# Attention on one core: probability transposes ahead of a group's first projections, the last query block's scores behind the projections

## The chip, the cores and the metric

The kernel runs on one core of a Trainium2 chip. The metric is the device time of one execution in microseconds; the lower, the better. The engines that matter here are TensorE (PE in the profile; its weight loads are PEld), VectorE (DVE), ScalarE (ACT), GpSimd (POOL) and SyncE (SP), which issues the loads.

## What is computed

One decoder layer in float32: self-attention, a cross-attention with a given context, and a mixture of experts. The change touches the self-attention alone:

```python
def proj(W):
    y = jnp.einsum('bsh,oh->bso', hidden_states, W)
    return y.reshape(B, S, NH, HD).transpose(0, 2, 1, 3)
q, k, v = (proj(Wq), proj(Wk), proj(Wv))
q = q * cos + rotate_half(q) * sin
k = k * cos + rotate_half(k) * sin
scores = jnp.einsum('bhqd,bhkd->bhqk', q, k) / math.sqrt(HD)
scores = jnp.where(causal, -jnp.inf, scores)
attn = jax.nn.softmax(scores, axis=-1)
out = jnp.einsum('bhqk,bhkd->bhqd', attn, v)
```

The batch is 4, the sequence 1024, the width 1024, with 16 heads of 64. `x` is normalised before it.

## The kernel before

`self_attention` works through 4 batches of 8 pairs of heads. Each engine has one queue, written by hand, and works it in order; semaphores tie the queues together. For every batch a `prologue` turns `x` and makes the first pair's projections. Then `attention` runs once for each pair, eight times in a batch: the first pair, three passes of a hardware loop (`pe.Fori`) with two pairs each, and the last pair. While it weighs the values of pair j it makes the projections of pair j + 1, except in the last pair of a batch. So 28 of the 32 calls have projections in them; these are the "pairs with projections" below.

Values are split in two float32r summands (`_hi` and `_lo`): ScalarE writes `_hi`, VectorE or GpSimd writes `_lo` as the rest, and TensorE multiplies both.

A pair has 24 steps, `STEPS[s] = (u, kb)`: unit u is a head and a half of the queries (`u` 0 to 3; two units see 4 key blocks of 128, two see 8), kb is the key block. A step does the following on TensorE, in this order:

- it turns the probabilities of key block kb (2 to 4 transposes, 1 at the diagonal's end; L433), to bank `ps_t`. ScalarE copies them to `pt_hi` (L556) and VectorE makes `pt_lo` (L707);
- it makes the scores of one query block of a later unit (`next_queries`, `scores`, L373 to L377), to `ps_s`. VectorE takes the row maxima (L659), ScalarE the exponentials (L494) and the normalisation (L502);
- it weighs the values (L417, L418) with the transposes of the step before. In the third step of a group this comes behind the projections.

Three steps are a group (`PER = 3`, `group, place = divmod(s, PER)`), and group t makes the projection of token block t of the next pair. Its 24 matmuls, 8 weight blocks k of 128 rows with three terms each (L347), are cut in `PARTS`: 12 at place 0, 6 at place 1 and 6 at place 2. All go to the one bank `ps_qkv`. When the last is done, ScalarE copies the value part (L481), and VectorE runs `rotate` (L632, L635, L636, L637, L642). The first projection of the next group waits for `qkv_read`, which L637 gives. At place 1 the rotated queries and keys of the block before are turned (L361), copied by ScalarE (L485) and split by VectorE (L650, L651).

In group 0 two more things happen. The weights of the next pair are only now being split: ScalarE writes `w_hi` (L472) of blocks 4 and 5 in step 0 and of blocks 6 and 7 in step 1 (`W_OF_STEP`), each block followed by `w_lo` on GpSimd (L276, `rest_of_w`), and the projections wait for it block by block:

```python
k, term = divmod(n, 3)
if t == 0 and term == 0:
    pe.wait_ge(w_lo_ok, START + j * HB + k + 1)
```

And the scores of step 2 are those of the last query block of unit 1. They need token block 7 of this pair's queries and keys, which is turned in step 1, so they wait for L651.

Of the kernel before, what the change touches and what calls it, by code (L numbers as in the profile page):

```python
# [113 lines left out]
def self_attention(nc, const, x, wqkv, cos, sin, attn_out):  # L114
# [10 lines left out]
    STEPS = [(u, kb) for u in range(NU) for kb in range(KB[u])]  # L125
    NS = len(STEPS)
    PER = NS // TB
# [12 lines left out]
    def next_queries(s, last):  # L140

        u, kb = STEPS[s]
        if KB[u] == GQ:
            then = [(u + 1, kb + 1)] if kb + 1 < GQ else []
        else:
            then = [(u + 1, kb // 2)] if kb % 2 == 0 else [(u + 2, 0)] if kb == KB[u] - 1 else []
        return [(unit // NU, unit % NU, i) for unit, i in then if unit < NU or not last]

    def tile_order(last):


        order = []
        for s in range(NS):
            order.append(("probs", s))
            if s % PER == 1 and (s < PER or not last):
                order.append(("qk", s // PER))
        return {key: i for i, key in enumerate(order)}

    with ExitStack() as scope:
# [46 lines left out]
        def first_tile(j):  # L206

            return j * NT + TB - 1
# [120 lines left out]
        def _(pe):  # L329
# [8 lines left out]
            def qkv(j, t, part, out):  # L338

                for n in part:  # L340
# [4 lines that stand above are left out]
                    a = slice(t * P, (t + 1) * P)  # L345
                    xs, ws = ((xt_hi, w_hi), (xt_hi, w_lo), (xt_lo, w_hi))[term]
                    mm = pe.matmul(out, xs[:, k, a], ws[:, k, :], start=(n == 0), stop=(n == 3 * HB - 1))  # L347
                    if t == TB - 1 and n == 3 * SLOTS - 1:

                        mm.then_inc(w_early, 1)  # L350
                if part[-1] == 3 * HB - 1:
                    mm.then_inc(qkv_ok, 1)

            def turn_qk(j, t, start, at):


                pe.wait_ge(rot_ok, START + j * TB + t + 1)

                pe.wait_ge(tile_lo_ok, START + (start + (at - 1 if at >= 2 else 0)))
                for r in range(4):  # L360
                    mm = pe.transpose(ps_t[:, at % 2, r * P:(r + 1) * P], rotated[:, r, :, :].rearrange("p a d -> p (a d)"), ident[:, :])  # L361
                mm.then_inc(tile_ok, 1)

            def scores(j, slot, u, i):
                h, g = UNITS[u]
                n = GQ * u + i
                qb = GQ * g + i
                keys = P * (qb + 1)
                for c in range(0, keys, BANK):

                    w = max(min(BANK, keys - c), 2 * P)
                    out = ps_s[:, n % 2, c:c + w]
                    pe.matmul(out, qk_hi[slot][:, h, qb * P:(qb + 1) * P], qk_hi[slot][:, 2 + h, c:c + w],  # L373
                              start=True, stop=False, skip_group_check=True)
                    pe.matmul(out, q_lo[slot][:, h, qb * P:(qb + 1) * P], qk_hi[slot][:, 2 + h, c:c + w],
                              start=False, stop=True, skip_group_check=True)
                mm = pe.matmul(ps_s[:, n % 2, qb * P:(qb + 1) * P], ident16[:, :], mask16[:, :],  # L377
                               start=False, stop=True, skip_group_check=True)
                mm.then_inc(s_ok, 1)
# [27 lines left out]
            def weigh_values(j, slot, s, tile):  # L407
                u, kb = STEPS[s]
                h, g = UNITS[u]

                pe.wait_ge(tile_lo_ok, START + tile)
                if kb == 0:

                    pe.wait_ge(o_ok, START + j * NU + u)
                off = P * max(0, kb - GQ * g)
                both = v[slot][:, kb, h, :, :].rearrange("p a d -> p (a d)")
                pe.matmul(ps_o[:, off:], both, pt_hi[:, s % 2, off:], start=(kb == 0), stop=False, skip_group_check=True)  # L417
                pe.matmul(ps_o[:, off:], both, pt_lo[:, s % 2, off:], start=False, stop=True,  # L418
                          skip_group_check=True).then_inc(pv_ok, 1)

            def attention(j, slot, first, last):
                tiles = tile_order(last)
                for s, (u, kb) in enumerate(STEPS):
                    h, g = UNITS[u]
                    group, place = divmod(s, PER)
                    if kb == 0:

                        pe.wait_ge(norm_ok, START + j * NQ + GQ * (u + 1))
                    at = tiles["probs", s]

                    pe.wait_ge(tile_lo_ok, START + first_tile(j) + (at - 1))
                    for i in range(max(0, kb - GQ * g), GQ):
                        mm = pe.transpose(ps_t[:, (TB - 1 + at) % 2, i * P:(i + 1) * P], probs[g][:, i, kb * P:(kb + 1) * P], ident[:, :])  # L433
                    mm.then_inc(tile_ok, 1)
                    for ahead, unit, i in next_queries(s, last):

                        if unit == 1 and not ahead:
                            pe.wait_ge(tile_lo_ok, START + (first_tile(j) + (tiles["qk", 0] + 1 if i == GQ - 1 else 0)))
                        elif unit == 1:
                            pe.wait_ge(tile_lo_ok, START + first_tile(j) + tiles["qk", GQ + 1] + 1)  # L440
                        elif unit == 0 and i == 0:
                            pe.wait_ge(tile_lo_ok, START + first_tile(j) + tiles["qk", GQ] + 1)

                        pe.wait_ge(exp_ok, START + (j + ahead) * NQ + GQ * unit + i - 1)
                        scores(j + ahead, (slot + ahead) % 2, unit, i)
                    if 0 < s and place < PER - 1:
                        weigh_values(j, slot, s - 1, first_tile(j) + tiles["probs", s - 1] + 1)
                    elif s == 0 and not first:
                        weigh_values(j - 1, 1 - slot, NS - 1, first_tile(j))
                    if place == 1 and group == 0:  # L450
                        turn_qk(j, TB - 1, j * NT, TB - 1 + tiles["qk", 0])
                    elif place == 1 and not last:
                        turn_qk(j + 1, group - 1, j * NT, TB - 1 + tiles["qk", group])
                    if not last:
                        if place == 0:

                            pe.wait_ge(qkv_read, START + j * TB + TB + group)
                        qkv(j + 1, group, PARTS[place], ps_qkv[:, 0:W])
                    if place == PER - 1:

                        weigh_values(j, slot, s - 1, first_tile(j) + tiles["probs", s - 1] + 1)

            def drain(j):
                weigh_values(j, 1, NS - 1, (j + 1) * NT)

            for_pairs(pe, prologue, attention, drain)

        @block.scalar
# [1655 lines left out]
```

## Time and profile before

| what | value |
| --- | --- |
| median of 3 runs (lowest to highest) | 7976.89 us (7974.31 to 7977.77) |
| the profiled execution's own time | 7973.0 us |
| its span | 7971.4 us |
| TensorE busy in the span | 7279.0 us (91%) |
| VectorE, ScalarE, GpSimd busy | 4039.8, 3494.3, 1726.8 us |
| attention, from the first pair's first step to the last batch's end | 83.0 to 2519.8 us of the span |
| TensorE busy in that stretch | 2194.49 us |
| a pair with projections, 850.5 to 920.1 us | 69.60 us |

Start times count from the start of the span. A busy time of TensorE contains the time that a matmul takes to run through the array: a 128x384 matmul is shown with 0.33 us, yet the next one starts 0.17 us after it. So waits are read best from the distance between starts, and a wait shorter than the run-through does not show as idle time on PE; the row of the weight load (PEld) may show it. "Clock 1.00" in a row is the full 2.4 GHz, 0.50 is 1.2 GHz.

### The profile page before, as it was taken

How to read it: one execution, taken by the hardware profiler on the slowest of the kernel's cores; microseconds unless marked ns; L12 is line 12 of the kernel's file. 1: busy time of each engine (PE TensorE's matmuls, PEld its weight loads, DVE VectorE, ACT ScalarE, POOL GpSimd, SP SyncE). 2: the span in 40 equal slices, each digit the busy share in tenths (PEclk: the TensorE clock that was granted, in tenths of full speed). 3: DMA queues.
4: the chain of work that ended last, by engine and by line, in shares of the span. 5: the costliest groups of instructions: out<-in, count | busy, mean ns of one | idle time of the engine just before them, and what ended most of it. 6: DMA issues, size and time to landing. Idle time of an engine off the chain costs nothing.

```text
span 7971.4 us, 127669 instructions
## 1 busy us (share of the span) xinstructions
PE 7279.0 (91%) x39854; PEld 6170.5 (77%) x39856; DVE 4039.8 (51%) x8063; ACT 3494.3 (44%) x6664; POOL 1726.8 (22%) x1646
## 2 busy tenths in 40 slices
PE   8998997997996988994899999999999999999999
PEld 7887886886885777773777888877887878887887
DVE  6666666666665444345444444444444444444444
ACT  5665665665665122110344444444444444444443
POOL 1111111111110000000233333333333333333333
PEclk9998998998998999996899999999999999999999
DMA  1101111111102111211455555555555555555555
GB/s 58 32 25 51 27 31 43 32 32 43 32 25 81 64 67 64 93 56 39 134 163 153 155 154 154 155 158 157 155 153 172 150 163 155 155 153 157 154 155 145
DMA packets 286465, 826.59 MB, mean 104 GB/s; under 512 B 35872, under 2 KB 103456, under 8 KB 286112
## 3 DMA queue, kind: packets, MB, share of 16 engines
q0 software_dynamic: 98928, 365.58, 18.9%
q1 hardware_dynamic: 187184, 456.61, 17.5%
q8 instruction: 185, 3.03, 0.2%
q14 instruction: 168, 1.38, 0.1%
HBM read 615.37 MB, written 206.70 MB: 103 GB/s over the span
## 4 chain that ended last, share of the span: by engine, by line
PE 44%; DMA 2%; issue 2%; DVE 1%; DVEq 1%; ACT 1%; POOLq 0%; ACTq 0%; POOL 0%
PE ps_gu L1612 9%; PE ps_gu L1614 9%; PE ps_gu L1613 9%; PE ps_y L1612 4%; PE ps_y L1614 4%; PE ps_y L1613 4%; PE ps_xe L1632 3%; DMA xt_rows<-rows,gather_t 2%; PE ps_xe L1641 1%; DVEq L1482 1%; PE ps_l L1621 1%; DVE gu_lo L1972 1%; POOLq L1482 0%; ACT y_last L1774 0%; ACT xs_hi L1757 0%
## 5 line engine op out<-in xcount | busy, mean ns | idle before, releaser
L1612 PE MATMUL ps_gu<-xs_hi,gu_hi 128*128 128x512 f32 x3072 | 1232.2, 401 | 95.0 <-DVE gu_lo L1972 95.0
L1614 PE MATMUL ps_gu<-xs_hi,gu_lo 128*128 128x512 f32 x3072 | 1213.0, 395 | 0.0
L1613 PE MATMUL ps_gu<-xs_lo,gu_hi 128*128 128x512 f32 x3072 | 1209.8, 394 | 0.0
L1612 PEld LDWEIGHTS ps_gu<-xs_hi,gu_hi 128*128 128x128 f32 x3072 | 583.0, 190 | 240.9 <-DVE gu_lo L1972 122.5
L347 PE MATMUL ps_qkv<-w_hi,xt_hi 128*128 128x384 f32 x1920 | 711.3, 370 | 51.9 <-DVE v L637 51.9
L1591 POOL TENSOR_TENSOR dn_lo<-raw_w,dn_hi 128x512 fp32r<-128x512 f32 x384 | 485.2, 1298 | 1007.8 <-ACT dn_hi L1793 1007.8
L1614 PEld LDWEIGHTS ps_gu<-xs_hi,gu_lo 128*128 128x128 f32 x3072 | 582.9, 190 | 131.1
L1613 PEld LDWEIGHTS ps_gu<-xs_lo,gu_hi 128*128 128x128 f32 x3072 | 583.2, 190 | 122.3
L707 DVE TENSOR_TENSOR pt_lo<-ps_t,pt_hi 128x512 fp32r<-128x512 f32 (+3 forms) x768 | 425.3, 554 | 451.7 <-ACT pt_hi L556 438.8
L347 PE MATMUL ps_qkv<-w_hi,xt_lo 128*128 128x384 f32 x1920 | 653.3, 340 | 0.0
L347 PE MATMUL ps_qkv<-w_lo,xt_hi 128*128 128x384 f32 x1920 | 651.5, 339 | 0.0
L1612 PE MATMUL ps_y<-dn_hi,hs_hi 128*128 128x512 f32 x1536 | 628.5, 409 | 0.0
L1972 DVE TENSOR_TENSOR gu_lo<-raw_w,gu_hi 128x512 fp32r<-128x512 f32 x768 | 485.1, 686 | 263.5 <-ACT gu_hi L1793 262.4
L1932 DVE TENSOR_TENSOR xs_lo<-ps_xe,xs_hi 128x512 fp32r<-128x512 f32 x520 | 334.6, 685 | 549.9 <-ACT xs_hi L1757 549.9
L1614 PE MATMUL ps_y<-dn_hi,hs_lo 128*128 128x512 f32 x1536 | 606.7, 395 | 0.0
L1613 PE MATMUL ps_y<-dn_lo,hs_hi 128*128 128x512 f32 x1536 | 606.2, 395 | 0.0
L1805 ACT ACTIVATE hs_hi<-act_s 128x512 fp32r<-128x512 f32 x192 | 121.3, 632 | 1096.6 <-DVE act_s L1977 1096.6
L1977 DVE TENSOR_TENSOR act_s<-ps_gu,act_s 128x512 f32<-128x512 f32 x192 | 132.9, 692 | 925.2 <-PE ps_gu L1614 925.2
L556 ACT ACTIVATE pt_hi<-ps_t 128x512 fp32r<-128x512 f32 (+3 forms) x768 | 374.9, 488 | 342.8 <-PE ps_t L433 324.9
L1569 POOL DMA_INDIRECT out<-y_sup,scatter_s x192 | 303.5, 1581 | 1003.7 <-ACT y_sup L1815 980.3
L1793 ACT ACTIVATE gu_hi<-raw_w 128x512 fp32r<-128x512 f32 x768 | 426.0, 618 | 184.2 <-DMA raw_w<-w_gu 184.2
L1815 ACT ACTIVATE y_sup<-ps_y,w_now 128x512 f32<-128x512 f32 x384 | 264.6, 689 | 437.8 <-PE ps_y L1614 422.5
(303 smaller groups left out, 16328.8 us busy)
## 6 DMA issues: line engine op xcount, KB each, us to landing
raw_w<-w_gu SPq DMA_DIRECT2D x384, 512.0 KB, 4.1
raw_w<-w_down SPq DMA_DIRECT2D x192, 512.0 KB, 6.7
w_raw<-wqkv SPq DMA_DIRECT2D x260, 192.0 KB, 2.5
out<-residual SPq DMA_DIRECT2D x36, 512.0 KB, 2.6
probs<-x SPq DMA_DIRECT2D x32, 512.0 KB, 3.4
attn_out<-out_t POOLq DMA_DIRECT2D x128, 128.0 KB, 2.2
residual<-x SPq DMA_DIRECT2D x32, 512.0 KB, 4.2
stage<-attn_out SPq DMA_DIRECT2D x32, 512.0 KB, 5.1
```

What stands on the lines that cost most here:

```text
L347: mm = pe.matmul(out, xs[:, k, a], ws[:, k, :], start=(n == 0), stop=(n == 3 * HB - 1))
L556: act.activation(pt_hi[:, s % 2, off:], ps_t[:, (TB - 1 + at) % 2, off:], ACT.Copy).then_inc(tile_hi_ok, 1)
L707: dve.tensor_tensor(pt_lo[:, s % 2, off:], ps_t[:, (TB - 1 + at) % 2, off:], raw(pt_hi[:, s % 2, off:]), ALU.subtract).then_inc(tile_lo_ok, 1)
L1569: pool.indirect_dma_start(out, bass.IndirectOffsetOnAxis(ap=scatter_s[:, i:i + 1], axis=0), y_sup[:, i % 2, :], None, compute_op=ALU.add). ...
L1591: pool.tensor_tensor(dn_lo[:, f, a], raw_w[:, f, a], raw(dn_hi[:, f, a]), ALU.subtract).then_inc(dn_lo_ok, 1)
L1612: pe.matmul(out, a_hi, w_hi, start=first, stop=False)
L1613: pe.matmul(out, a_hi, w_lo, start=False, stop=False)
L1614: return pe.matmul(out, a_lo, w_hi, start=False, stop=last)
L1793: act.activation(dst[:, a], raw_w[:, c % RING, a], ACT.Copy).then_inc(hi_ok, 1)
L1815: act.activation(y_sup[:, i % 2, a], ps_y[:, a], ACT.Copy, scale=w_now[:, i:i + 1]).then_inc(ys_ok, 1)
L1932: dve.tensor_tensor(xs_lo[:, ks, a], ps_x1[:, c * BANK:(c + 1) * BANK].rearrange("p (k c) -> p k c", c=P), raw(xs_hi[:, ks, a]), ALU.subtr ...
L1972: dve.tensor_tensor(gu_lo[:, c // 2, b], raw_w[:, c % RING, a], raw(gu_hi[:, c // 2, b]), ALU.subtract).then_inc(lo_ok, 1)
```

## The change

The body of `attention` on TensorE gets two local functions, `turn_probs(s)` (the transposes) and `next_scores(s)` (the scores), with the same instructions as before. Two orders change, both in the 28 pairs with projections:

- `turned_early(s)`: the transposes of the second step of a group are issued in the first step, ahead of the group's 12 first projections and of their wait for `qkv_read`. That holds for six of the eight groups (steps 1, 7, 10, 13, 19, 22). Steps 4 and 16 start a unit (kb = 0) and stay.
- `late_scores`: in step 2 the scores go behind the six projections, so that they come between these and the weighing of values.

The queues of the other engines are the same as before, instruction by instruction.

```diff
@@ -420,9 +420,10 @@
 
             def attention(j, slot, first, last):
                 tiles = tile_order(last)
-                for s, (u, kb) in enumerate(STEPS):
+
+                def turn_probs(s):
+                    u, kb = STEPS[s]
                     h, g = UNITS[u]
-                    group, place = divmod(s, PER)
                     if kb == 0:
 
                         pe.wait_ge(norm_ok, START + j * NQ + GQ * (u + 1))
@@ -432,6 +433,8 @@
                     for i in range(max(0, kb - GQ * g), GQ):
                         mm = pe.transpose(ps_t[:, (TB - 1 + at) % 2, i * P:(i + 1) * P], probs[g][:, i, kb * P:(kb + 1) * P], ident[:, :])
                     mm.then_inc(tile_ok, 1)
+
+                def next_scores(s):
                     for ahead, unit, i in next_queries(s, last):
 
                         if unit == 1 and not ahead:
@@ -443,6 +446,18 @@
 
                         pe.wait_ge(exp_ok, START + (j + ahead) * NQ + GQ * unit + i - 1)
                         scores(j + ahead, (slot + ahead) % 2, unit, i)
+
+                def turned_early(s):
+
+                    return not last and s % PER == 1 and STEPS[s][1] > 0
+
+                for s, (u, kb) in enumerate(STEPS):
+                    group, place = divmod(s, PER)
+                    if not turned_early(s):
+                        turn_probs(s)
+                    late_scores = group == 0 and place == PER - 1 and not last
+                    if not late_scores:
+                        next_scores(s)
                     if 0 < s and place < PER - 1:
                         weigh_values(j, slot, s - 1, first_tile(j) + tiles["probs", s - 1] + 1)
                     elif s == 0 and not first:
@@ -454,8 +469,12 @@
                     if not last:
                         if place == 0:
 
+                            if turned_early(s + 1):
+                                turn_probs(s + 1)
                             pe.wait_ge(qkv_read, START + j * TB + TB + group)
                         qkv(j + 1, group, PARTS[place], ps_qkv[:, 0:W])
+                    if late_scores:
+                        next_scores(s)
                     if place == PER - 1:
 
                         weigh_values(j, slot, s - 1, first_tile(j) + tiles["probs", s - 1] + 1)
```

On TensorE's queue, step 2 of a pair in the loop: `ps_t<-ident,probs` are the transposes, `ps_s` the scores, `ps_qkv` the projections, of weight blocks 6 and 7 here. Before:

```order
L433 MATMUL ps_t<-ident,probs 128x128 x2
L438 REGISTER_ALU
L444 REGISTER_ALU
L373 MATMUL ps_s<-qk_hi 128x512
L375 MATMUL ps_s<-qk_hi,q_lo 128x512
L373 MATMUL ps_s<-qk_hi 128x512
L375 MATMUL ps_s<-qk_hi,q_lo 128x512
L377 MATMUL ps_s<-mask,ident 128x128
L344 REGISTER_ALU
L347 MATMUL ps_qkv<-w_hi,xt_hi 128x384
L347 MATMUL ps_qkv<-w_lo,xt_hi 128x384
L347 MATMUL ps_qkv<-w_hi,xt_lo 128x384
```

And after the change:

```order
L434 MATMUL ps_t<-ident,probs 128x128 x2
L344 REGISTER_ALU
L347 MATMUL ps_qkv<-w_hi,xt_hi 128x384
L347 MATMUL ps_qkv<-w_lo,xt_hi 128x384
L347 MATMUL ps_qkv<-w_hi,xt_lo 128x384
L344 REGISTER_ALU
L347 MATMUL ps_qkv<-w_hi,xt_hi 128x384
L347 MATMUL ps_qkv<-w_lo,xt_hi 128x384
L347 MATMUL ps_qkv<-w_hi,xt_lo 128x384
L441 REGISTER_ALU
L447 REGISTER_ALU
L373 MATMUL ps_s<-qk_hi 128x512
```

The projections of block 6 and, three rows on, of block 7 (each with its wait for `w_lo_ok`) now stand ahead of the scores.

On the same queue, steps 6 and 7 of the pair: `ps_o` is the weighing of values, and the register operation ahead of the projections belongs to the wait for `qkv_read`. Before:

```order
L411 REGISTER_ALU
L417 MATMUL ps_o<-pt_hi,v 128x512
L418 MATMUL ps_o<-pt_lo,v 128x512
L457 REGISTER_ALU
L347 MATMUL ps_qkv<-w_hi,xt_hi 128x384
L347 MATMUL ps_qkv<-w_lo,xt_hi 128x384
...
L347 MATMUL ps_qkv<-w_hi,xt_lo 128x384
L433 MATMUL ps_t<-ident,probs 128x128 x4
L411 REGISTER_ALU
L417 MATMUL ps_o<-pt_hi,v 128x512
```

And after the change:

```order
L411 REGISTER_ALU
L417 MATMUL ps_o<-pt_hi,v 128x512
L418 MATMUL ps_o<-pt_lo,v 128x512
L434 MATMUL ps_t<-ident,probs 128x128 x4
L474 REGISTER_ALU
L347 MATMUL ps_qkv<-w_hi,xt_hi 128x384
L347 MATMUL ps_qkv<-w_lo,xt_hi 128x384
...
L347 MATMUL ps_qkv<-w_hi,xt_lo 128x384
L411 REGISTER_ALU
L417 MATMUL ps_o<-pt_hi,v 128x512
```

The four transposes of step 7 moved from behind the twelve projections to ahead of them and of their wait. Steps 9 and 10 read the same way with two transposes, steps 18, 19 and 21, 22 repeat them in the second half.

## Rows read from the trace of the kernel before

**Rows 1.** Who waited for whom, 0 to 2560 us: total us, times, longest.

```profile
PEld ps_qkv L347 <- DVE v L637: 106.1, 168, 1.0
...
PE ps_o L417 <- DVE out_t L671: 30.3, 22, 2.4
PE ps_s L373 <- DVE qk_hi L651: 29.5, 29, 1.4
...
PEld ps_qkv L347 <- POOL w_lo L276: 0.9, 3, 0.4
```

**Rows 2.** Windows: length, busy of five engines, clock, DMA share, GB/s.

```profile
850.50:920.10 69.60, 66.57 (x408) 59.60 (x408) 47.92 (x117) 47.17 (x102) 10.44 (x12) 1.00 0.12 31
2318.20:2390.80 72.60, 68.28 (x409) 61.17 (x409) 47.24 (x114) 46.48 (x100) 10.25 (x12) 0.98 0.11 29
436.80:510.70 73.90, 69.64 (x408) 61.78 (x408) 47.14 (x114) 46.21 (x100) 10.10 (x12) 0.95 0.10 28
2325.00:2328.50 3.50, 2.86 (x10) 2.57 (x11) 2.15 (x4) 3.48 (x8) 1.97 (x2) 0.60 0.19 56
```

**Rows 3.** Timeline of PE, steps 6 and 7: start, length, instruction.

```profile
870.42 0.39 PE L418 MATMUL ps_o<-pt_lo,v 128*128 128x512 f32 x1
870.99 0.34 PE L347 MATMUL ps_qkv<-w_lo,xt_hi 128*128 128x384 f32 x1
...
872.73 0.34 PE L347 MATMUL ps_qkv<-w_hi,xt_lo 128*128 128x384 f32 x1
872.91 0.60 PE L433 MATMUL ps_t<-ident,probs 128*128 128x128 f32 x4
873.26 0.48 PE L417 MATMUL ps_o<-pt_hi,v 128*128 128x512 f32 x1
873.58 0.39 PE L418 MATMUL ps_o<-pt_lo,v 128*128 128x512 f32 x1
873.81 0.60 PE L361 MATMUL ps_t<-ident,rotated 128*128 128x128 f32 x4
```

**Rows 4.** Timeline of PE, steps 9 and 10 of the same pair.

```profile
878.30 0.40 PE L418 MATMUL ps_o<-pt_lo,v 128*128 128x512 f32 x1
878.86 0.45 PE L347 MATMUL ps_qkv<-w_hi,xt_hi 128*128 128x384 f32 x1 [0.16 <-DVE v L637]
879.15 0.34 PE L347 MATMUL ps_qkv<-w_lo,xt_hi 128*128 128x384 f32 x1
...
880.88 0.34 PE L347 MATMUL ps_qkv<-w_hi,xt_lo 128*128 128x384 f32 x1
881.06 0.38 PE L433 MATMUL ps_t<-ident,probs 128*128 128x128 f32 x2
...
881.51 0.40 PE L375 MATMUL ps_s<-qk_hi,q_lo 128*128 128x512 f32 x1
```

**Rows 5.** Timeline of PE, steps 2 and 3 of the same pair.

```profile
857.39 0.38 PE L433 MATMUL ps_t<-ident,probs 128*128 128x128 f32 x2
858.89 0.49 PE L373 MATMUL ps_s<-qk_hi 128*128 128x512 f32 x1 [1.11 <-DVE qk_hi L651]
...
859.91 0.23 PE L377 MATMUL ps_s<-mask,ident 128*128 128x128 bf16 x1
859.95 0.42 PE L347 MATMUL ps_qkv<-w_hi,xt_hi 128*128 128x384 f32 x1
...
861.67 0.28 PE L418 MATMUL ps_o<-pt_lo,v 128*128 128x256 f32 x1
862.76 0.44 PE L347 MATMUL ps_qkv<-w_hi,xt_hi 128*128 128x384 f32 x1 [0.81 <-DVE v L637]
```

**Rows 6.** Timeline of POOL, 850 to 864 us: the rests of weight blocks.

```profile
858.27 1.97 POOL L276 TENSOR_TENSOR w_lo<-w_raw,w_hi 128x384 fp32r<-128x384 f32 x2 [1.63 <-ACT w_hi L472]
```

**Rows 7.** Timeline of DVE, step 2: maxima, then rotation.

```profile
860.28 1.21 DVE L659 TENSOR_REDUCE neg_max<-ps_s 128x1 f32<-128x1024 f32 x1
861.69 0.42 DVE L632 TENSOR_TENSOR r_cos<-ps_qkv,cos_sb 128x256 f32<-128x256 f32 x1 [0.19 <-ACT v L481]
```

## The prediction

> **What bounds the kernel now.** I read first the table of who waited for whom, cut to the attention stretch, because the change moves waits and adds no work. It shows which waits TensorE has left [rows 1]. Its first projections of a group wait for the rotation, which frees `ps_qkv`: 168 waits of a weight load, 106.1 us, six in each of the 28 pairs with projections. The scores of step 2 wait for L651 29 times, 29.5 us in all. For the weights' rests on GpSimd it hardly waits at all: 3 times, 0.9 us. That row is the one to keep in mind, because it is a cover and not a freedom.
>
> Then the windows [rows 2]. A pair takes 69.60 us, of which TensorE is busy 66.57, so the stage is TensorE's own work plus short waits, and what can be won is those waits. Pairs behind a jump of the hardware loop are longer and have a lower clock: 0.98 and 0.95.
>
> Last the timelines of one pair at full clock, where I take the distance from start to start. Without a wait, the matmul behind L418 (512 columns) starts 0.23 us after it (873.58 to 873.81), and a projection 0.17 us after another [rows 3].
>
> **Transposes ahead, steps 6 and 7 (and 18 and 19).** From L418 at 870.42 to the second projection at 870.99 there are 0.57 us; without a wait it would be 0.23 + 0.17 = 0.40 [rows 3]. So the wait costs 0.17. Where the transposes stand now, from the last projection (872.73) over them to L418 (873.58), there are 0.85 us; without them the way is 0.17 + 0.23 = 0.40. Taking them away there saves 0.45. In front they need the 0.23 behind L418, 0.35 for themselves (872.91 to 873.26), and about 0.26 to the second projection (an estimate between 0.17 and the 0.28 that a projection behind a wait takes to the next): 0.84 instead of 0.57, so 0.27 is paid. Net 0.18, which is the wait. The bounds are 0.17 and 0.28.
>
> **Steps 9 and 10 (and 21 and 22).** Here L418 at 878.30 to the second projection at 879.15 is 0.85 us, a wait worth 0.45 [rows 4]. Two transposes take at most the 0.35 of four, so they vanish in it whole, and the projections start as before. Behind, 880.88 to the second scores at 881.51 is 0.63, against 0.17 + 0.23 = 0.40 without them: 0.23 saved.
>
> **Steps 0 and 1, 12 and 13.** Same move, but I count 0. The rows of waits give six waits for the rotation to a pair, and eight groups; the two groups in which other work already covers it are these two by their place behind the scores of a whole block. Transposes in front cost there what they save behind. Steps 3 and 15 have the long waits (below), but their next transposes start a unit and do not move, so nothing fills them.
>
> The early transposes add no wait of their own: they need the bank that L707 has read, and the weighing of values just ahead of them needs the same L707. ScalarE's copies of them can only come sooner.
>
> Sum of this part: 2 x 0.18 + 2 x 0.23 = 0.82 us a pair, 28 pairs: 23 us gained.
>
> **What a rule would make of it.** The transposes of rows 3 start 0.11 us apart. The Trainium skill, "TensorE: Matmul & The Clock Gate", section "Back-to-back issue gap", gives N/2.4 + 2.5 ns for isolated matmuls at full clock, 56 ns at 128 columns. By it, two transposes would hide 0.11 us instead of 0.23, and the part would bring an estimated 0.56 us a pair, 16 us. The rows have the duration of this very form, so I stay with them.
>
> **Scores behind the projections, step 2.** Now the transposes start at 857.39, the scores at 858.89 after an idle 1.11 us, their last matmul (the mask) at 859.91, the projections at 859.95 [rows 5]. It looks as if the six projections, some 1.04 us, would fit that hole. But they are of weight blocks 6 and 7, and they wait for `w_lo_ok`. GpSimd makes these two rests from 858.27 on, 1.97 us together, and was itself idle until ScalarE gave it the `w_hi` [rows 6]: the first is ready at about 859.26, the second at 860.24. Before the change the wait for L651 and the scores covered this: the projections of block 6 started at 859.95, 0.7 us after their weights.
>
> After the change, with the weights at the same times: block 6 starts at about 859.3, block 7 not before 860.3. From there 0.28 + 0.17 + 0.17 us to the first score matmul [rows 3] gives 860.9, although L651 would have let it go at 858.89. The mask comes 0.23 x 4 behind (the spacing of 512 columns), at about 861.9 instead of 859.91.
>
> What is queued behind: VectorE's row maxima of 1024 keys. They start 0.37 us after the mask and last 1.21 [rows 5, 7]; behind them on the same queue stands the rotation (L632), and behind its L637 the first projection of group 1, 1.07 us after L632 starts (861.69 to 862.76). So: 861.9 + 0.37 + 1.21 = 863.4 for L632, less a few hundredths of overlap, and 864.5 for the projection instead of 862.76. TensorE has only the weighing, one transpose and the weighing again to do meanwhile, which now end at 861.67 [rows 5] and would end near 862.5. Each pair loses 864.50 - 862.76 = **1.74 us**.
>
> Bounds: a gain of 0.2 if the weights came early enough, because then L632 would start with the end of the maxima at 861.49 and not at 861.69; a loss of 2.0 if the whole delay of the mask went through. The value comes from the chain, since each link has a row. Nothing later takes it up: TensorE is the engine that others follow from step 4 on.
>
> Three pairs are like the one with clock 0.95 [rows 2]: I take it that their step 2 runs partly at half clock and their rotation is late already, and count nothing for them. 25 x 1.74 = 43.5 us lost.
>
> **Sum.** 43.5 - 23 = 20.5 us slower. The profiled execution's own time is 7973.0 us, 3.9 below the median of the runs shown; 7973.0 + 20.5 + 3.9 = 7997.4. I predict 7997 us.
>
> **Rivals.**
> 1. *The clock falls in the new waits* (later than 8008). In step 2 TensorE now stands still from 857.5 (the second transpose, 0.11 us behind 857.39) to 859.3, and ahead of group 1 from 862.5 to 864.5: 1.8 and 2.0 us, where it stood 1.4 and 1.1. The longest wait for L671 was 2.4 us [rows 1], and in the window just behind such a one the clock is 0.60 [rows 2]. Against it: the pair at 850.5 has waits of 1.4 us and clock 1.00. The price: TensorE is busy 68.28 us in a pair with clock 0.98 against 66.57, 1.7 us; ten such pairs are 17 us, all 28 are 48. The Trainium skill, same page, section "Part 4: PE-mode transpose", says that transposes do not count as busy for the clock gate; by that rule the transposes placed beside these waits would not help the clock, and it speaks for this rival; no row of this trace tells transposes apart there. Chance 0.18.
> 2. *Loss and gain nearly cancel* (7961 to 7993). If ScalarE and GpSimd run 0.7 us earlier in step 1, since its transposes are there sooner, the delay shrinks to 1.0 us: 25 - 23 = 2 us slower. Against it: GpSimd waits 1.63 us for ScalarE ahead of those blocks, so it is ScalarE that would have to be faster, and its queue has the exponentials and copies ahead in the same order. Chance 0.18.
> 3. *Faster* (below 7961). The wait for the weights does not come because block 7 is ready when its projections are. Then step 2 brings 0.2 us a pair, 5 us, and the first part its 23: 7977 - 28 = 7949. It decides at one point: the rest of block 7 must be done by about 858.1 (857.5 + 0.6), and the row has 860.24. For a gain over 16 us with the first part alone the delay must stay under 0.25 us a pair. Chance 0.09.
>
> **Numbers.** My forecast (7990 to 8008) has 0.55. A measurement of this kernel tells 0.2%, 16 us, from no change. Of the forecast's range a small piece lies under +16 us: slower 0.55 - 0.05 + 0.18 = 0.68, same 0.23, faster 0.09. The range for 8 in 10 takes in most of rivals 1 and 2: 7974 to 8028. Its lower end is a delay of 0.8 us a pair, its upper end 18 pairs with a lower clock.
>
> **What the trace after would show.** The row "PEld ps_qkv L347 <- POOL w_lo L276" rises from 0.9 us to some 40 or more, with about two waits a pair. The wait of L373 for L651 goes from 29 times to four or so, those of the last pairs. The waits for L637 fall to about four a pair and grow at group 1. The pair that took 69.60 us takes 70.5. Steps 6, 7 and 9, 10 show no or a shorter wait at the projections. I am wrong if the weights' wait stays small, if group 1's projection is not late, or if the clock in pairs without a jump leaves 1.00.

## The result and the profile after

The changed kernel takes 8007.12 us (median of 6 runs, 7996.88 to 8008.32) against 7976.9 us (6 runs, 7974.01 to 7986.96): 1.0035 times the time before, with a 95% interval of 1.0024 to 1.0047. That ratio is 28 us; the two medians lie 30 us apart. Its profiled execution took 7996.88 us, the shortest of the six and 23.9 us more than the profiled one of before.

Between these two profiled executions all of the difference lies in attention. The first matmul of the next stage starts at 2589.33 us of the span; it started at 2565.02. That is 24.3 us, and behind it the two programs take the same (5406.0 and 5406.4 us). In the kernel after, L637 has become L656, L651 L670, L659 L678, L632 L651, L433 L434, L472 L491; the lines of the attention's other matmuls have kept their numbers. Some kernels of the experiments have a few lines more: in the timelines of stand_in_weights and rests_last L350 and L349 are L347, L376 and L375 (with `ps_s<-qk_hi`) are L373, and the L659 that two waits for the rotation name is L637.

The table of who waited for whom, 0 to 2600 us of the changed kernel (total us, times, longest), answers to [rows 1]:

```profile
PEld ps_qkv L347 <- DVE v L656: 78.7, 112, 1.7
PEld ps_qkv L347 <- POOL w_lo L276: 65.1, 63, 1.9
...
PE ps_o L417 <- DVE out_t L690: 35.1, 24, 2.6
...
PE ps_s L373 <- DVE qk_hi L670: 5.4, 4, 1.4
```

The waits for the rotation fall from 168 to 112, four a pair, but the longest grows from 1.0 to 1.7 us. The scores' wait is left only in the four last pairs. In its place stands the wait for the weights' rests on GpSimd: 65.1 us where there was 0.9. The wait for the rotation and that of the scores have lost 27.4 and 24.1 us, and the new wait has brought 64.2.

The same pair as in [rows 5], PE's timeline of steps 2 and 3; the pair starts at 859.20 instead of 850.52:

```profile
866.03 0.38 PE L434 MATMUL ps_t<-ident,probs 128*128 128x128 f32 x2
868.00 0.45 PE L347 MATMUL ps_qkv<-w_hi,xt_hi 128*128 128x384 f32 x1 [1.59 <-POOL w_lo L276]
...
868.98 0.44 PE L347 MATMUL ps_qkv<-w_hi,xt_hi 128*128 128x384 f32 x1 [0.18 <-POOL w_lo L276]
...
869.62 0.40 PE L373 MATMUL ps_s<-qk_hi 128*128 128x512 f32 x1
...
870.55 0.23 PE L377 MATMUL ps_s<-mask,ident 128*128 128x128 bf16 x1
...
871.25 0.28 PE L418 MATMUL ps_o<-pt_lo,v 128*128 128x256 f32 x1
873.02 0.44 PE L347 MATMUL ps_qkv<-w_hi,xt_hi 128*128 128x384 f32 x1 [1.49 <-DVE v L656]
```

And POOL's and DVE's timelines there, which answer to [rows 6, 7]:

```profile
866.96 1.96 POOL L276 TENSOR_TENSOR w_lo<-w_raw,w_hi 128x384 fp32r<-128x384 f32 x2 [1.63 <-ACT w_hi L491]
...
870.82 1.23 DVE L678 TENSOR_REDUCE neg_max<-ps_s 128x1 f32<-128x1024 f32 x1 [1.76 <-PE ps_s L377]
871.96 0.41 DVE L651 TENSOR_TENSOR r_cos<-ps_qkv,cos_sb 128x256 f32<-128x256 f32 x1
```

Read them from the pair's start. The rests begin 7.76 us into the pair, as before (7.75), with the same idle 1.63 ahead: GpSimd and ScalarE are not a bit earlier. Block 6's projection stands at 8.80, its rest being done at about 7.76 + 0.98 = 8.74; block 7's at 9.78, its rest at 9.72. The mask starts at 11.35 instead of 9.39, the maxima at 11.62 instead of 9.76, the first projection of group 1 at 13.82 instead of 12.24. So group 1 starts 1.58 us late.

Now the windows of a pair at full clock, the one that starts at 1135.53 before. Length, busy of five engines, clock, DMA share, GB/s; first the kernel before, then the changed one:

```profile
1135.53:1205.15 69.62, 66.61 (x408) 59.62 (x409) 47.91 (x117) 47.15 (x102) 10.45 (x12) 1.00 0.11 31
```

```profile
1149.40:1219.67 70.27, 66.20 (x408) 59.79 (x409) 48.07 (x117) 47.03 (x102) 10.45 (x12) 1.00 0.11 31
```

The pair is 0.65 us longer with the same 408 matmuls, and TensorE is busy 0.41 us less, at clock 1.00. That is waiting, and 28 times 0.65 is 18 of the 24 us.

### The profile page after: what moved, and what is told of

The parts are those of the page before. It is cut to its first block, busy times and chain, and to the rows that moved or that the text cites. A ratio compares the mean times of both kernels' runs of the same rounds, so it can differ in the third digit from the quotient of the medians.

```text
span 7995.3 us, 127670 instructions
## 1 busy us (share of the span) xinstructions
PE 7272.3 (91%) x39855; PEld 6173.9 (77%) x39856; DVE 4044.8 (51%) x8063; ACT 3488.4 (44%) x6664; POOL 1728.0 (22%) x1646
## 4 chain that ended last, share of the span: by engine, by line
PE 44%; DMA 2%; issue 2%; DVE 1%; DVEq 1%; ACT 1%; POOLq 0%; ACTq 0%; POOL 0%
PE ps_gu L1631 9%; PE ps_gu L1633 9%; PE ps_gu L1632 9%; PE ps_y L1631 4%; PE ps_y L1633 4%; PE ps_y L1632 4%; PE ps_xe L1651 3%; DMA xt_rows<-rows,gather_t 2%; PE ps_xe L1660 1%; DVEq L1501 1%; PE ps_l L1640 1%; DVE gu_lo L1991 1%; POOLq L1501 0%; ACT y_last L1793 0%; ACT xs_hi L1776 0%
## 5 line engine op out<-in xcount | busy, mean ns | idle before, releaser
L347 PE MATMUL ps_qkv<-w_hi,xt_hi 128*128 128x384 f32 x1920 | 711.5, 371 | 103.5 <-DVE v L656 56.5
L347 PE MATMUL ps_qkv<-w_lo,xt_hi 128*128 128x384 f32 x1920 | 647.0, 337 | 0.0
L347 PE MATMUL ps_qkv<-w_hi,xt_lo 128*128 128x384 f32 x1920 | 646.8, 337 | 0.0
L347 PEld LDWEIGHTS ps_qkv<-w_hi,xt_hi 128*128 128x128 f32 x1920 | 364.4, 190 | 144.2 <-DVE v L656 78.7
```

## Experiments

Each kernel is compared with runs of the kernel before on the same chip (7979.04 us for the first four, 7978.34 for the next four, 7977.31 for the last). "Next stage" is the start of its first matmul in the profiled execution; "pair" is the length of a pair at full clock, from its first transposes to those of the next pair; "half clock" is the time at 0.50 in us in the 28 pairs with projections, without the stretch at 0.50 in which the first pair of each batch begins. "Hit" counts the pairs with a stretch at 0.50 among 16: the second, third, fifth and seventh of each batch, which have none in the kernel before.

| kernel | median us | ratio (95%) | next stage | pair | half clock | hit |
| --- | --- | --- | --- | --- | --- | --- |
| before | 7976.9 | 1 | 2565.0 | 69.62 | 37.5 | 0 |
| changed | 8007.12 | 1.0035 (1.0024 to 1.0047) | 2589.3 | 70.27 | 41.0 | 4 |
| changed_again | 8006.0 | 1.003 (1.0018 to 1.0042) | 2595.6 | 70.26 | 51.2 | 5 |
| early_turns_alone | 7956.16 | 0.9971 (0.9961 to 0.9981) | 2541.5 | 68.68 | 20.5 | 0 |
| late_scores_alone | 8039.83 | 1.0077 (1.0063 to 1.0091) | 2623.9 | 71.13 | 58.0 | 8 |
| stand_in_weights | 7979.2 | 1.0 (0.9991 to 1.0009) | 2536.4 | 68.45 | 17.1 | 0 |
| scores_between | 7971.34 | 0.9994 (0.9985 to 1.0003) | 2559.2 | 69.30 | 10.2 | 0 |
| rests_last | 7987.47 | 1.0011 (1.0002 to 1.002) | 2572.1 | 69.95 | 27.3 | 1 |
| filled_waits | 8023.35 | 1.0056 (1.0042 to 1.007) | 2583.8 | 70.22 | 3.4 | 0 |
| turns_1_13 | 7978.2 | 0.9999 (0.999 to 1.0008) | 2565.7 | 69.55 | 20.5 | 0 |
| rotation_first | 8006.39 | 1.0038 (1.0024 to 1.0051) | 2583.6 | 70.24 | 37.5 | 2 |

Behind the attention no kernel has a changed order. Yet that stretch varies from one profiled execution to the next, from 5406.0 us (changed) to 5416.3 (changed_again) where the experts get the right tokens, so two single executions can differ by some 10 us there without a cause in the change; "next stage" and "pair" leave that out.

My theory: the late scores uncover the weights' wait, and it reaches group 1 through the row maxima; the early transposes gain by themselves. Rivals: the clock falls in the new waits, or the early transposes are what costs.

**early_turns_alone.** The changed kernel without the late scores.

```diff
-                    late_scores = group == 0 and place == PER - 1 and not last
+                    late_scores = False
```

> The changed kernel with the scores of step 2 back ahead of the projections; the transposes stay ahead. My sum: 0.82 us gained in each of 28 pairs, so 23 us below the kernel before, about 7954; a pair at full clock goes from 69.60 to about 68.8. By the transposes' price of 56 ns it would be 16 us, about 7961. If the gain of this part were only a rounding of waits, 7977.

It is 23 us faster than before. Its timeline of PE, steps 6 and 7, then 9 and 10 of the pair that starts at 842.77, beside [rows 3, 4]:

```profile
862.67 0.39 PE L418 MATMUL ps_o<-pt_lo,v 128*128 128x512 f32 x1
862.90 0.60 PE L434 MATMUL ps_t<-ident,probs 128*128 128x128 f32 x4
...
863.51 0.33 PE L347 MATMUL ps_qkv<-w_lo,xt_hi 128*128 128x384 f32 x1
...
865.27 0.33 PE L347 MATMUL ps_qkv<-w_hi,xt_lo 128*128 128x384 f32 x1
865.45 0.39 PE L417 MATMUL ps_o<-pt_hi,v 128*128 128x512 f32 x1
865.67 0.39 PE L418 MATMUL ps_o<-pt_lo,v 128*128 128x512 f32 x1
...
870.39 0.39 PE L418 MATMUL ps_o<-pt_lo,v 128*128 128x512 f32 x1
870.63 0.38 PE L434 MATMUL ps_t<-ident,probs 128*128 128x128 f32 x2
...
871.22 0.34 PE L347 MATMUL ps_qkv<-w_lo,xt_hi 128*128 128x384 f32 x1
...
872.98 0.33 PE L347 MATMUL ps_qkv<-w_hi,xt_lo 128*128 128x384 f32 x1
873.15 0.39 PE L373 MATMUL ps_s<-qk_hi 128*128 128x512 f32 x1
873.38 0.40 PE L375 MATMUL ps_s<-qk_hi,q_lo 128*128 128x512 f32 x1
```

From L418 to the second projection: 0.84 where it was 0.57, and 0.83 where it was 0.85. Behind, 0.40 instead of 0.85, and 0.40 instead of 0.63. These are the four distances of the prediction, to 0.02 us.

**late_scores_alone.** The other half: `turned_early` always answers no.

```diff
-                    return not last and s % PER == 1 and STEPS[s][1] > 0
+                    return False
```

> The changed kernel with the transposes back behind the projections; the scores of step 2 stay behind them. Weights' theory: 1.6 to 1.7 us lost in some 25 pairs, 40 to 44 us, about 8019, and more if the clock falls in further pairs. A theory by which late scores cost nothing of their own and the two moves hurt each other says 7977.

61 us slower; 40 to 44 us were expected, and more if the clock falls. The pair at full clock is 1.51 us longer; with the 0.94 that the other half gains, the sum is +0.57, against +0.65 for both together. So in a pair without a fall of the clock the halves add, to 0.08 us. The whole times don't (61 - 23 = 38, measured 28 to 30). A part of that is the clock. Of these windows the first is a pair that has a fall, up to its last matmul, the second the fall, which lies on block 7's projections and the scores:

```profile
868.70:940.60 71.90, 67.92 (x406) 60.44 (x407) 47.41 (x117) 46.67 (x100) 10.15 (x12) 0.98 0.11 30
878.60:882.00 3.40, 3.40 (x10) 2.67 (x11) 0.43 (x1) 0.84 (x2) 0.30 (x1) 0.50 0.55 154
```

From the first score matmul to the mask there are 1.71 us in this pair instead of 0.93, in the very chain that is late. Of the 16 pairs of the kinds that had no fall before (the second, third, fifth and seventh of a batch), 8 have one here. But in the profiles the 28 pairs together add nearly as the halves do: 54.1 us more here and 27.1 less in early_turns_alone make 27.0, and both together have 24.1 (28.5 in changed_again). The rest of the mismatch lies in attention outside these pairs, which took 4.8 and 3.6 us longer than before in the two halves and 0.2 with both (2.0 in changed_again). The order there is that of before; why it takes longer stays open.

**stand_in_weights.** The changed kernel, where step 2 of group 0 multiplies with weight blocks 4 and 5 in place of 6 and 7, and the wait for 6 and 7 comes at group 1. So part of the projections is computed with other weights, and the experts get other tokens; only the attention stretch compares.

```diff
-                    if t == 0 and term == 0:
+                    if late and t == 0 and k >= 6:
+                        k -= 2
+                    elif t == 0 and term == 0:
                         pe.wait_ge(w_lo_ok, START + j * HB + k + 1)
+                    if late and t == 1 and n == 0:
+                        pe.wait_ge(w_lo_ok, START + j * HB + HB)
...
```

> Both moves, but the projections of step 2 in group 0 read weight blocks 4 and 5 once more in place of 6 and 7 (so the computation is changed there), for whose rests the step before has already waited; the wait for blocks 6 and 7 is made at group 1. Same work, same order, no wait for weights. Weights' theory: the scores start when L651 lets them, 0.2 us a pair is gained there, all together about 7949. A theory by which the order itself is at fault (scores behind 1.04 us of projections hold up the maxima) says no better than 7990.

The median, 7979.2 us where about 7949 was expected, contains the other tokens: what follows the attention takes 5438.8 us of the profile instead of 5406.4. Attention ends 28.6 us earlier than before: without the weights' wait the change is a gain, and the sum of the prediction's rival 3 (23 + 5) comes out. With the wait the falls of the clock in the 16 pairs are gone too. PE's timeline of step 2, pair start 843.63:

```profile
852.00 0.49 PE L376 MATMUL ps_s<-qk_hi 128*128 128x512 f32 x1
...
853.02 0.23 PE L380 MATMUL ps_s<-mask,ident 128*128 128x128 bf16 x1
...
853.76 0.28 PE L421 MATMUL ps_o<-pt_lo,v 128*128 128x256 f32 x1
855.66 0.43 PE L350 MATMUL ps_qkv<-w_hi,xt_hi 128*128 128x384 f32 x1 [1.63 <-DVE v L659]
```

It also shows why so little was to be had. The scores start 8.37 us into the pair, as before (8.37), since L651's work (here L673) lets them go no sooner: in both kernels it ends 0.13 us ahead of them. The hole of 1.11 us is filled, but a hole of 1.63 stands ahead of group 1, where there was 0.81: the first projection comes at 12.03 instead of 12.24. Filling the one hole moved the waiting to the next.

**scores_between.** The scores between the projections of block 6 and block 7.

```diff
-                        qkv(j + 1, group, PARTS[place], ps_qkv[:, 0:W])
-                    if late_scores:
-                        next_scores(s)
+                        if late_scores:
+                            qkv(j + 1, group, PARTS[place][:3], ps_qkv[:, 0:W])
+                            next_scores(s)
+                            qkv(j + 1, group, PARTS[place][3:], ps_qkv[:, 0:W])
+                        else:
+                            qkv(j + 1, group, PARTS[place], ps_qkv[:, 0:W])
```

> Both moves, but the scores of step 2 stand between the projections of block 6 and those of block 7. They then wait for the first rest only, 0.98 us less: the first projection of group 1 comes 0.9 to 1.0 us earlier than in the changed kernel. Weights' theory: 25 us below the changed kernel, about 7977 to 7982. If the clock is most of the loss, the fall is larger; if not the weights but the length of the projections counts, it is half a microsecond a pair, 14 us.

7971.34 us, 6 us below the expected range. The pair is 0.97 us shorter than in the changed kernel, 27 us in 28 pairs; the time at half clock falls from 41.0 to 10.2 us with it. With one block's wait ahead, PE's timeline has

```profile
857.74 0.45 PE L347 MATMUL ps_qkv<-w_hi,xt_hi 128*128 128x384 f32 x1 [1.58 <-POOL w_lo L276]
...
859.30 0.23 PE L377 MATMUL ps_s<-mask,ident 128*128 128x128 bf16 x1
859.33 0.42 PE L347 MATMUL ps_qkv<-w_hi,xt_hi 128*128 128x384 f32 x1
...
861.77 0.44 PE L347 MATMUL ps_qkv<-w_hi,xt_hi 128*128 128x384 f32 x1 [0.96 <-DVE v L659]
```

The pair starts at 848.94: the mask at 10.36 is 0.97 late, and group 1 at 12.83 is 0.59 late. Each block that stands ahead of the scores adds its share (0.59 for one, 1.58 for two), as the chain wants it.

**rests_last.** In the changed kernel's step 2 the two terms of each block that need only `w_hi` go first, the two `w_lo` terms last.

```diff
-                for n in part:
+                order = sorted(part, key=lambda n: n % 3 == 1) if rests_last else part
+                for n in order:
                     k, term = divmod(n, 3)
-                    if t == 0 and term == 0:
+                    if rests_last and term == 0:
+                        pe.wait_ge(w_hi_ok, START + j * HB + k + 1)
+                    if t == 0 and term == (1 if rests_last else 0):
...
```

> Both moves, and the six projections of step 2 in group 0 in another order: the four that need only the upper parts of blocks 6 and 7 first, the two with the rests last. In the changed kernel the fourth projection waits for block 7's rest and two more follow it; here one follows none behind that rest. Weights' theory: the scores start 0.45 us sooner (0.28 + 0.17), 28 pairs, 12 us below the changed kernel, and the wait behind the transposes is shorter by a microsecond, so the clock falls less often, which may bring up to 10 us more: 7985 to 7995. If the clock were no part of it, 7995. If not the last rest but the first sets the start, a microsecond a pair, 28 us.

The pair is 0.32 us shorter than the changed one, less than the 0.45 expected, and the time 7987.47, 19 us below the changed kernel. The same six matmuls in the same place, only ordered by when their weights come, win that much. The wait for block 7's rest ends where it did, 9.78 us into the pair (it starts at 854.25), but one projection is left behind it and not three:

```profile
862.67 0.34 PE L349 MATMUL ps_qkv<-w_hi,xt_lo 128*128 128x384 f32 x1
863.07 0.44 PE L349 MATMUL ps_qkv<-w_lo,xt_hi 128*128 128x384 f32 x1
864.03 0.45 PE L349 MATMUL ps_qkv<-w_lo,xt_hi 128*128 128x384 f32 x1 [0.52 <-POOL w_lo L276]
864.31 0.48 PE L375 MATMUL ps_s<-qk_hi 128*128 128x512 f32 x1
```

So the scores start at 10.06 instead of 10.42. The expected 0.45 us took one of the two projections saved at 0.28; both stand in a stream, at 0.17 or 0.18.

**filled_waits.** For the clock: 12 small bf16 matmuls into columns 384 to 511 of `ps_qkv` ahead of step 2's projections. They spoil what the bank has gathered, so the projections' values and the experts' tokens are others, and again only the attention stretch compares.

```diff
+            def fill(n):
+                for _ in range(n):
+                    pe.matmul(ps_qkv[:, W:BANK], ident16[:, :], mask16[:, :], start=True, stop=True,
+                              skip_group_check=True)
...
+                        if late_scores:
+                            fill(12)
                         qkv(j + 1, group, PARTS[place], ps_qkv[:, 0:W])
```

> The changed kernel with 12 more small matmuls, written to unused columns of the projections' bank, in the 1.8 us that TensorE stands still ahead of the projections of step 2. They add work and take no wait away. The weights still come when they come, so a pair at full clock stays at 70.25 us. Clock theory: the falls in the pairs without a loop jump (4 of 16 in the trace of the changed kernel, 8 of 16 with the late scores alone) go away, and the median falls from 8007 to 7995 to 8000. If the clock has no part in it: 8007 or a few us later, since in the pairs behind a jump the wait is only 0.6 us and the fillers delay the projections by 0.7.

The fillers take 0.83 us of the wait and delay nothing: the pair at full clock stays at 70.22. In a pair behind a jump, where the expectation feared a delay, they ended at 938.91 and the first projection started at 939.86. But the half clock in the 28 pairs goes from 41.0 us to 3.4, and the 28 pairs together take 2000.7 us, against 2011.0 in the changed kernel's first profile and 2015.5 in its second. So all falls together cost the changed kernel 10 to 15 us. Not all of that is the change's, since the kernel before has falls too (37.5 us at half clock). Without nearly all of them the 28 pairs are still 13.7 us longer than the 1986.9 of before: the falls alone don't make the loss. The median, 8023.35 us where 7995 to 8000 was expected, says nothing of this: the stretch behind the attention took 5435.7 us with the other tokens.

**turns_1_13.** Only the transposes of steps 1 and 13 ahead, no late scores.

```diff
-                    return not last and s % PER == 1 and STEPS[s][1] > 0
+                    return not last and s in (1, 13)
...
-                    late_scores = group == 0 and place == PER - 1 and not last
+                    late_scores = False
```

> The kernel before with only the transposes of steps 1 and 13 moved ahead of the first projections, where I counted no gain and no loss: 7977 within 2, a pair at 69.6. If moving transposes has a price or a gain of its own apart from the waits for L637, it shows here, 0.1 us being 3 us in all.

0.9999 (0.999 to 1.0008), and the second and seventh pairs of the batches, which run at full clock, are the same to 0.03 us on average. The move counts 0 there.

**changed_again.** The changed kernel unaltered, for a second profile.

> The changed kernel once more, for a second trace, since the execution profiled first (7997) is 10 us below its median (8007). Clock theory: if this execution is near 8007, its trace has more falls of the clock near 10 us into the pairs than the 4 of 16 of the first one, each worth 0.6 to 1 us, and the pairs without a fall are still at 70.25. Else the pairs without a fall are longer themselves, or the time is outside the attention.

8006.0 us. The profiled execution took 8013.43, 16.5 us more than the changed kernel's first profile. Of these, 6.2 us lie in attention (more time at half clock, the full pairs as long as before) and 10.3 behind it, where the order is the same: 5416.3 against 5406.0 us, with 358 and 343 us at half clock. So the third case of the expectation holds for the larger part. Its windows hold the worst case of the clock, a pair and the stretch inside it:

```profile
2054.45:2126.68 72.23, 68.84 (x408) 61.96 (x408) 48.04 (x117) 46.85 (x102) 10.43 (x12) 0.95 0.11 30
2065.20:2072.00 6.80, 5.95 (x20) 4.93 (x19) 3.01 (x8) 2.63 (x5) 0.00 (x0) 0.50 0.18 51
```

The same pair took 70.25 us in the first profile. 6.8 us at half clock cost 2.0; stretches of 3.4 us cost between 0.6 and 1.4 in the second and seventh pairs of the batches. Which pairs are hit differs from one execution to the next (5 of the 16 here, 4 in the first profile).

**rotation_first.** To test the last link: in step 2 VectorE makes the four operations that read `ps_qkv` ahead of the maxima, and the sum behind them.

```diff
...
+                for args in between:
+                    maxima(*args)
                 dve.wait_ge(rot_step, START + n * 3 + 3)
...
-                        maxima(j + ahead, unit, i)
+                        if s != PER - 1 or last:
+                            maxima(j + ahead, unit, i)
...
-                        rotate(j + 1, 1 - slot, group, ps_qkv, first_tile(j) + tiles["qk", group] + 1)
+                        rotate(j + 1, 1 - slot, group, ps_qkv, first_tile(j) + tiles["qk", group] + 1,
+                               fresh if group == 0 else ())
```

> The changed kernel, in which VectorE, in step 2 of the 28 pairs with projections, makes the four operations of the rotation that read ps_qkv ahead of the row maxima of 1024 keys, and the sum (rotated) behind them. The theory of the chain: the weights' wait and the scores stand as they did, but the maxima (1.23 us) no longer lie between the mask and the first projection of group 1. The last projection of group 0 starts at 869.43 in the changed kernel's trace, ScalarE's copy of the values ends at 870.1, the rotation takes 1.0 us, so the projection of group 1 starts at about 871.4 instead of 873.02, 12.2 us into the pair instead of 13.8. The maxima then end near 872.2 instead of 872.05, the exponentials and the normalisation (1.11, 0.3 and 1.16 us) end near 875.0 instead of 874.8, and the transposes of step 4, which read them and would stand at 873.6, wait for ScalarE until about 875.0 instead of 875.24. So the wait moves and 0.2 us a pair is left: some 6 us faster than the changed kernel, about 7995 to 8003 us, with a new wait of ps_t for probs of about 1.4 us, 25 to 28 times. Rival (the maxima are no link, the first projection of group 1 is held by the projections' end or ScalarE's queue): it stays near 13.8 us into the pair and the time is the changed kernel's. Second rival (the new wait lets the clock fall): slower than the changed kernel, with stretches at 0.5 about 14 to 16 us into a pair.

PE's timeline, pair start 855.91:

```profile
867.26 0.23 PE L377 MATMUL ps_s<-mask,ident 128*128 128x128 bf16 x1
...
867.96 0.28 PE L418 MATMUL ps_o<-pt_lo,v 128*128 128x256 f32 x1
868.08 0.36 PE L347 MATMUL ps_qkv<-w_hi,xt_hi 128*128 128x384 f32 x1
...
870.04 0.34 PE L347 MATMUL ps_qkv<-w_hi,xt_lo 128*128 128x384 f32 x1
871.87 0.65 PE L434 MATMUL ps_t<-ident,probs 128*128 128x128 f32 x4 [1.49 <-ACT probs L521]
```

The mask is as late as ever (11.35), yet group 1's first projection starts at 12.17 instead of 13.82, behind its weighing without a wait. So the maxima were the link. The wait comes back at the transposes of step 4, which need these very scores' probabilities: they start at 15.96, and stood at 16.04 in the changed kernel. 0.08 us is left of the 0.2 expected, and the median is the changed kernel's, not the 7995 to 8003 that was expected. There are two ways from the mask to TensorE, and the second is nearly as long as the first.

## Why the prediction was right

**The forecast.** 7997 us was predicted, 8007 measured, inside the range, on the side to which most of the chance was given. Against its own profile the prediction looks closer, +20.5 in the sum and +23.9 measured, but that is luck: this execution was the shortest of six. The medians are 30 us apart, and the second profile is 40 us above that of before, 10 of them behind the attention. The sum had no term for new falls of the clock. At full clock 28 pairs lose 18.2 us, a little less than the 20.5 of the sum; in the two profiles they lost 24.1 and 28.5.

**The wait for the weights: shown.** GpSimd's start, both blocks, the scores and the mask stand where the chain put them (859.3, 860.9 and 861.9 in the prediction are 8.8, 10.4 and 11.4 us into a pair that starts at 850.52; block 6, the scores and the mask stand at 8.80, 10.42 and 11.35). The row of this wait rose to 65.1 us with 63 waits, the scores wait for L670 four times, and the rotation four times a pair, as the prediction had it. stand_in_weights takes this wait away, and with it the falls; at full clock, where no falls are in play, the first projection of group 1 is then 0.21 us early instead of 1.58 late, the small gain that the lower bound had.

**The term of 1.74 us was 1.58.** Two gaps of VectorE were sized wrongly. The maxima start 0.27 us behind the mask, not the 0.37 of [rows 5, 7], and the rotation starts 0.09 us before they end. The late part alone costs 1.51 in a full pair.

**The early transposes: 0.82 predicted, 0.94 measured.** By the rows, steps 6/7 came to 0.18 and steps 9/10 to 0.25. The rest, some 0.1, is spread over the pair in pieces of 0.05 or less; steps 12 and 13 have one of them. What holds it was not followed further. The two transposes of step 10 gave back 0.23 us, 0.11 each. The Trainium skill, "TensorE: Matmul & The Clock Gate", section "Back-to-back issue gap", has 56 ns at 128 columns for isolated matmuls, and about 81 ns for a stream with weight loads. The measurement decides: the float32 transposes in the stream here cost more than either.

**The three pairs counted as nothing: wrong, but small.** I took it that the late scores cost nothing in the three pairs with clock 0.95, and gave these pairs the gain of the transposes. They are the sixth of batch 1 and the fourth of batches 3 and 4. Together they are 0.1 us longer in the changed kernel's first profile and 0.9 shorter in the second, where the transposes alone would have made them 2.8 shorter (3 x 0.94). So the late scores cost them 1.0 and 0.6 us each, less than elsewhere but not nothing, 2 to 3 us in the sum. Nor are pairs behind a jump of the loop spared as a kind: the fourth and sixth pairs are together 9.8 us longer over the four batches, 1.2 each, more than the 0.65 of a pair at full clock. Summed by place in the batch every place loses; singly 25 of the 28 pairs do.

The other sizes were off both ways. By the pairs at full clock, the late scores cost 28 x 1.51 = 42.3 us (43.5 predicted) and the transposes gain 28 x 0.94 = 26.3 (23 predicted).

**Rival 1 was partly true beside the forecast, and I had set them as alternatives.** The clock does fall in new places, about 10 us into a pair, just behind the wait for the weights. That the clock leaves 1.00 in pairs without a jump was one of the prediction's own signs of being wrong, and it came in 4 and 5 of 16 pairs. Taking the 18.2 us of full-clock pairs from the 24.1 and 28.5 that the 28 pairs lost in the two profiles leaves 6 and 10 us for it and for the pairs behind the jumps, where the two can't be told apart; filled_waits puts all falls together at 10 to 15. The price I set, 1.7 us for each, was mostly too high (0.6 to 1.4 measured), and of the 16 pairs that had no fall about one in four is hit. The Trainium skill, same page, section "Part 4: PE-mode transpose", has it that a transpose doesn't count as busy for the clock gate in the same way; no run here tells them apart from the others: in every kernel with the late scores both sorts of work are missing in the same hole. The falls left in pairs behind a jump were there before the change, and their cause stays open.

**Rivals 2 and 3: refuted for this kernel.** ScalarE and GpSimd were not earlier at all (7.76 against 7.75 us), and block 7 was not ready.

## What to carry to other kernels

A hole ahead of an instruction may be what covers the next one's operands. Before work is pulled into it, look up when that work's own inputs are ready, not only whether it fits by length; a row of nearly no waiting (0.9 us here) can mean covered, not free. Then follow the moved instruction to the engines that wait for it along every path: putting right one of two nearly equal chains (rotation_first) brings nothing. A change of two parts should be timed by parts: the one part here is a gain of 23 us, 0.9971 (0.9961 to 0.9981), and by itself the best kernel of this study.

## What the runs showed of the hardware

Behind a wait of 1.6 us TensorE's granted clock fell from 1.00 to 0.50 (2.4 to 1.2 GHz) in some pairs and not in others of the same program. The length of the wait alone doesn't decide it: stand_in_weights has 1.63 us of it once in each pair and no fall in the 16 pairs in which the changed kernel has 4. scores_between has the same wait for the weights, 1.58 us, and no fall in the 16 either; there the wait ahead of group 1 is 0.96 us, where the changed kernel has 1.49. What decides it stays open. Twelve bf16 matmuls of 128 columns, 0.83 us of work in the wait, took away nearly all falls (41.0 to 3.4 us at half clock), also most of those behind the loop's jumps.

A projection behind a wait is followed by the next one 0.27 us later, where it is 0.17 in a stream (868.98 to 869.25 in the changed kernel). That is not a price of waiting: directly behind transposes, without a wait, it is 0.25 (863.26 to 863.51 in early_turns_alone), and directly behind the mask 0.26 (859.33 to 859.59 in scores_between). Why the second comes later there no run shows.
